# Layer 1 as seven products of quarters: W0 reloaded per batch, lora_a held still

## What is computed

```
Wc[b] = W0^T + I + coeff[b] * (2 * mask[b] - 1)         (1024 x 1024, per batch)
y[b]  = x[b] @ Wc[b] + b0                               (256 x 1024)
h[b]  = 2 * (y[b] @ lora_A[slot[b]])                    (256 x 16)
z[b]  = y[b] @ (W1^T + I) + b1 + h[b] @ lora_B[slot[b]] (256 x 1024)
```

## Time and profile before

| | |
|---|---|
| median of 3 runs | 392.09 us (392.07 to 392.19) |
| the profiled execution | 392.74 us |
| its span, first to last instruction | 390.9 us |
| instructions | 5982, of which 2334 matmuls |
| granted TensorE clock | 1.00 of full speed |
| moved by DMA | 61.76 MB, mean 158 GB/s |

### The profile page before, as it was taken

One profiled execution on the slowest core, in us unless ns is written; L12 is line 12 of the kernel. 1 busy time (PEld: TensorE's weight loads), 2 busy tenths in 40 slices (PEclk: granted clock), 3 DMA queues, 4 the chain that ended last, 5 costly groups with the idle time before them and its releaser, 6 DMA issues.

```text
span 390.9 us, 5982 instructions
## 1 busy us (share of the span) xinstructions
PE 382.0 (98%) x2334; PEld 359.1 (92%) x2334; DVE 245.9 (63%) x299; ACT 178.1 (46%) x313; POOL 49.7 (13%) x44
## 2 busy tenths in 40 slices
PE   8879999999999999999999999999999999999997
PEld 8879998998989999989999899899998999998996
DVE  3978989997177932788437981579617794281200
ACT  3546946656155622556235651464515563252221
POOL 2235910020003000030000300012000300002000
DMA  8999817873544633544526436164253562001011
GB/s 288 409 397 364 305 48 223 293 219 108 195 115 161 190 81 135 162 147 157 171 60 196 150 104 216 59 215 140 65 202 111 167 186 106 6 2 54 2 54 55
DMA packets 28078, 61.76 MB, mean 158 GB/s; under 512 B 2554, under 2 KB 3730, under 8 KB 28050
## 3 DMA queue, kind: packets, MB, share of 16 engines
q1 hardware_dynamic: 25232, 52.70, 41.6%
q10 hardware_dynamic: 2754, 8.66, 5.6%
q0 software_dynamic: 64, 0.01, 0.0%
HBM read 52.97 MB, written 8.39 MB: 157 GB/s over the span
## 4 chain that ended last, share of the span: by engine, by line
PE 83%; DVE 6%; DMA 4%; issue 3%; ACT 2%; SPq 1%; ACTq 0%; DVEq 0%
PE z_ps L385 43%; PE y_ps L347 23%; PE y_ps L353 12%; DMA ring<-in_mask 4%; DVE ring L680 3%; PE y_ps L385 2%; PE z_ps L429 2%; DVE wc_lo L688 2%; ACT wc_hi L499 1%; PE y_ps L317 1%; PE y_ps L327 1%; DVE y_two L727 0%; PE t_ps L420 0%; DVE y_raw L721 0%; ACT z_rows L552 0%
## 5 line engine op out<-in xcount | busy, mean ns | idle before, releaser
L385 PE MATMUL z_ps<-w_hi,y_two 128*128 128x344 f32 (+1 forms) x736 | 184.0, 323 | 1.3 <-DVE y_two L727 0.7
L385 PEld LDWEIGHTS z_ps<-w_hi,y_two 128*128 128x128 f32 x736 | 129.5, 188 | 3.0 <-DVE y_two L727 1.0
L347 PE MATMUL y_ps<-x_two,wc_hi 128*128 128x512 f32 x448 | 127.5, 395 | 0.0
L688 DVE SCALAR_TENSOR_TENSOR wc_lo<-ring,coeff_neg,wc_hi 128x1024 fp32r<-128x1024 f32 (+1 forms) x67 | 92.5, 1381 | 47.3 <-ACT wc_hi L499 46.5
L385 PE MATMUL z_ps<-w_lo,y_two 128*128 128x344 f32 (+1 forms) x368 | 118.3, 321 | 0.0
L499 ACT ACTIVATE wc_hi<-ring,coeff_neg 128x1024 fp32r<-128x1024 f32 (+1 forms) x67 | 74.6, 1115 | 71.5 <-PE y_ps L353 37.3
L680 DVE SCALAR_TENSOR_TENSOR ring<-ring,coeff_two,w_t 128x1024 f32<-128x1024 int32 (+1 forms) x67 | 86.6, 1301 | 8.2 <-DMA ring<-in_mask 7.3
L347 PEld LDWEIGHTS y_ps<-x_two,wc_hi 128*128 128x128 f32 x448 | 78.1, 189 | 10.9
L353 PEld LDWEIGHTS y_ps<-x_two,wc_lo 128*128 128x128 f32 x448 | 70.9, 189 | 8.4
L353 PE MATMUL y_ps<-x_two,wc_lo 128*128 128x256 f32 x448 | 78.2, 281 | 0.0
L385 PEld LDWEIGHTS z_ps<-w_lo,y_two 128*128 128x128 f32 x368 | 69.3, 188 | 0.0
(11 more groups left out here) (49 smaller groups left out, 182.3 us busy)
## 6 DMA issues: line engine op xcount, KB each, us to landing
ring<-in_mask SPq DMA_DIRECT2D x63, 512.0 KB, 4.4
x_raw<-in_x SPq DMA_DIRECT2D x31, 256.0 KB, 6.3
out<-z_rows ACTq DMA_DIRECT2D x15, 512.0 KB, 3.2
w_raw<-in_w SPq DMA_DIRECT2D x8, 512.0 KB, 10.3
w_t<-in_w SPq DMA_DIRECT2D x7, 512.0 KB, 9.3
b_raw<-in_lora_b SPq DMA_DIRECT2D x8, 256.0 KB, 3.6
w_t<-in_w SPq DMA_DIRECT2D x2, 256.0 KB, 3.7
ring<-in_mask SPq DMA_DIRECT2D x2, 256.0 KB, 4.8
```

The source lines that it names most:

```text
L347: pe.matmul(y_ps[o % HT][:, 0:2 * T], w, x_two[:, k, :, :], start=(k == 0), stop=False, skip_group_check=True)
L385: ins = pe.matmul(z_bank(b, s, g)[:, 0:EDGES[g + 1] - EDGES[g]], ys[:, k, s * P:(s + 1) * P], w[:, k, EDGES[g]:EDGES[g + 1]], start=(k == ...
L688: dve.scalar_tensor_tensor(out=wc_lo[:, k % RING, lo:hi], in0=sums[:, mask_entry(b, k) % RING, lo:hi], scalar=coeff_neg[:, b:b + 1], in1=w ...
```

## The change

- **Layer 1 from batch 2 on** (`winograd(b)`, FIRST = 2): y and W1 are cut in quarters of 128 or 512 by 512, and the four quarters of z are made of seven products instead of eight (Strassen's scheme in Winograd's form). Names: y quarters Y11, Y21, Y12, Y22, sums S1 = Y21 + Y22, S3 = Y11 - Y21, S2 = Y22 - S3, S4 = Y12 - S2; weight quarters W11 to W22 and T1 to T4, made once of quarters of W1 that are loaded again. V12 stands for the split Y12.
- **Batches 0 and 1** use plain products, but in halves of 512 columns (4 banks: 2 row halves x 2 column halves) instead of three groups.
- **h**: lora_a, high and low side by side, stands still (32 columns) and y moves, so h comes out turned (`low_rank`); `turn_h` and its copies are gone. In a seven-product batch h is made of Y11 with S1 times lora_a's upper half, Y12 times its lower half, and Y22 times their difference. lora_b is stacked seven times (112 rows) instead of four.
- **W0** isn't kept: each unit's piece of W0 is loaded with its mask into a ring of 6 slots, the sum is made in the mask's place, the high part in W0's place, the low part in the mask's. A slot is free when TensorE has used the unit; SP waits for that. Diagonals are raised for units 0, 1, 6 and 7 of every batch, two 128 x 128 blocks each.
- **PSUM**: two sets of four banks change places from half to half.
- **The lists** of all engines are written anew around this; `z_copy` of the seven-product batches becomes three `p_copy` on ScalarE, one `p_add` and four `z_add` on VectorE.

The diff, cut to its core (new functions as they are called):

```diff
-RING = 4
+RING = 6
@@ sync
-            def load_mask(b, k):
-                e = mask_entry(b, k)
+            def load_weights(b, k):
+
+                e = entry(b, k)
                 if e >= RING:
-
-                    sp.wait_ge(wc_lo_done, parts(0, e - RING))
+                    block_read(sp, b, k - RING)
...
+                    sp.dma_start(slot(w0_at, e), w0_u[:, ks, cols]).then_inc(w0_in[e % RING], 16)
+                    sp.dma_start(slot(mask_at, e), mask_u[b][:, ks, cols]).then_inc(ring_in[e % RING], 16)
...
             def load_x(b, g):
-                need(sp, x_lo_done, XG * (b - 1) + g + 1)
+                if b > 0:
+                    block_read(sp, b - 1, KT - 1)
...
+                need(sp, z_full, 4 * b)
+                sp.dma_start(b_raw[0:B_ALL, :], lora_b[bass.ds(slot, 1)].rearrange("a r o -> (a r) o")).then_inc(b_in, 16)
...
             for b in range(1, NB):
+                before = PAIR if b == 1 else HT
+                for u in range(before):
+                    load_weights(b, u)
                 for g in range(XG):
                     load_x(b, g)
...
+                for u in range(before, RING):
+                    load_weights(b, u)
+                if b == FIRST:
+
+                    sp.wait_ge(w12_read, 1)
+                    for c in range(2):
+                        load_t(T3, c, 1, W22, t_in[T3, c])
+                        load_t(T3, c, 0, W12, t_other_in[T3, c])
+                    load_lora(b)
+                if b == 1:
+
+                    for c in range(2):
+                        load_t(T1, c, 1, W12, t_in[T1, c])
+                        load_t(T1, c, 0, W11, t_other_in[T1, c])
+                        load_t(T2, c, 1, W22, t_in[T2, c])
+                        load_t(T4, c, 1, W21, t_in[T4, c])
+                    load_lora(b)
+                elif b > FIRST:
+                    load_lora(b)
+                for u in range(RING, KT):
+                    load_weights(b, u)
@@ gpsimd
+                w0_diagonal(b, KT - 2)
+                w0_diagonal(b, KT - 1)
+                if b + 1 < NB:
+                    w0_diagonal(b + 1, 0)
+                    w0_diagonal(b + 1, 1)
+                lora_a_diff(b)
                 lora_a_low(b)
-                lora_b_low(b)
+                lora_b_low(b, 0)
+                lora_b_low(b, 1)
@@ tensor
+            def product(bank, q, j, k, start):
+
+                for n, (yp, wp) in enumerate(((0, 0), (0, 1), (1, 0))):
+                    ins = pe.matmul(bank[:], y_two[:, q, k, yp, :], w1_two[wp][:, j, k, :],
+                                    start=(start and k == 0 and n == 0), stop=False, skip_group_check=True)
+                return ins
...
+            def low_rank(hs, q, a, k, start):
+                return pe.matmul(hs, a_parts[:, a, :, :], y_two[:, q, k, :, :], start=start, stop=False,
+                                 skip_group_check=True)
...
+                whole(X, Y11, W11, True).then_inc(p_full, 1)
+                pe.wait_ge(t_lo_done, t_count(T3, 1))
+                whole(V, S3, T3, True).then_inc(p_full, 1)
+                whole(W, V12, W21, True)
+
+                pe.wait_ge(p_copied, copied + 2)
+                whole(V, Y22, T4, False)
+                pe.wait_ge(y_lo_done, y_parts(b, S1))
+                pe.wait_ge(y_sum_done, KT * (b - 1) + HT + 1)
+                winograd_low_rank(b)
+
+                whole(Y, S1, T1, True).then_inc(p_full, 1)
+                pe.wait_ge(p_copied, copied + 1)
+                whole(X, S2, T2, False).then_inc(p_full, 1)
+                close(b, W)
+                close(b, V)
+
+                pe.wait_ge(y_lo_done, y_parts(b, S4))
+                pe.wait_ge(p_added, b - FIRST + 1)
+                for k in range(HT):
+                    product(layer1_bank(b, Y), S4, W22, k, False)
...
@@ scalar, batches from 2 on
+                    weights_high(b, KT - 2)
+                    store(b - 1, 0)
+                    store(b - 1, 1)
+                    for o in range(HT):
+                        y_copy(b, o)
+                    weights_high(b, KT - 1)
+                if winograd(b):
+                    y_high(b, Y11)
+                    y_high(b, S3)
...
                 lora_b_high(b)
+                lora_b_copy(b, 0)
                 if b + 1 < NB:
+                    weights_high(b + 1, 0)
+                    weights_high(b + 1, 1)
+                lora_a_high(b)
 
                 for o in range(HT, KT):
                     y_copy(b, o)
@@ vector, batches from 2 on
+                    weights_sum(b, KT - 2)
+                    weights_low(b, KT - 2)
+                    for o in range(HT):
+                        y_sum(b, o)
+                    weights_sum(b, KT - 1)
+                    y_add(b, S3)
+                    weights_low(b, KT - 1)
+                    y_low(b, Y11)
+                    y_low(b, S3)
                 if b + 1 < NB:
                     weights_sum(b + 1, 0)
+                    step(b + 1, 0)
+                    weights_low(b + 1, 1)
...
                 for o in range(HT, KT):
                     y_sum(b, o)
+                if winograd(b):
+                    y_add(b, S1)
+                    y_low(b, V12)
+                    y_add(b, S2)
+                    y_low(b, Y22)
+                    y_low(b, S1)
+                    y_add(b, S4)
+                    y_low(b, S2)
+                    y_low(b, S4)
+                    if b + 1 < NB:
+                        weights_sum(b + 1, PAIR)
+                        x_low(b + 1, 0)
+                        step(b + 1, PAIR)
+                        x_low(b + 1, 1)
+                        weights_low(b + 1, HT - 1)
+                    h_low(b)
+                    if b + 1 < NB:
+                        x_low(b + 1, 2)
+                        x_low(b + 1, 3)
+                    p_add(b)
+                    if b + 1 < NB:
+                        weights_sum(b + 1, HT)
+                        weights_sum(b + 1, HT + 1)
+                    z_add(b, W)
+                    if b + 1 < NB:
+                        weights_low(b + 1, HT)
+                    z_add(b, V)
+                    if b + 1 < NB:
+                        weights_low(b + 1, HT + 1)
+                    z_add(b, X)
+                    z_add(b, Y)
```

More of the change, by code:

```diff
@@ L34, in cond_residual_two_layers @@
     HALVED = 3
-    assert PAIR * T == BANK and PAIR == 2 and ST == 2 and XG == 4 and LR == 64 and KT == 2 * RING and NB > 2
+    FIRST = 2
+    B_HI, B_ALL = 6 * R, 7 * R
+    assert PAIR * T == BANK == HALF and PAIR == 2 and ST == 2 and XG == 4 and R == 16
+    assert HT < RING < KT and FIRST == 2 and NB > FIRST + 1
+    Y11, Y21, Y12, Y22 = range(4)
+    S1, S4, V12, S3, S2 = 1, 2, 4, 5, 6
+    Y_ORDER = (Y11, S3, V12, Y22, S1, S2, S4)
+    W11, W12, W21, W22, T1, T2, T4 = range(7)
+    T3 = W12
+    T_ORDER = ((T1, 0), (T2, 0), (T4, 0), (T1, 1), (T2, 1), (T4, 1), (T3, 0), (T3, 1))
     with ExitStack() as ctx:
@@ L73, in cond_residual_two_layers @@
[L73 to L78, removed]
+        a_raw = sb("a_raw", [P, KT + HT, R], F32)
+        a_parts = sb("a_parts", [P, KT + HT, 2, R], F32R)
+        h_stack = sb("h_stack", [P, T], F32R)
@@ L473, in layer1_last @@
-            def layer1_last(b):
-                layer1_group(b, 1, 2)
-                close_group(b, 1, 2)
+                for k in range(KT):
+                    if k == KT - 1:
+                        pe.wait_ge(y_lo_done, y_parts(0, k))
+                        plain_low_rank(0)
+                    pe.wait_ge(w1_lo_done, k + 1)
+                    pe.wait_ge(y_lo_done, y_parts(0, k))
+                    for i in range(4):
+                        plain(0, i, k)
+                for i in range(4):
+                    close(0, i)
@@ new lines, in z_copy, with store @@
+            def z_copy(b, i):
+                act.wait_ge(z_full, 4 * b + z_place(b, i))
+                s, _ = z_rows_of(b, i)
+                need(act, z_out[s], 16 * b)
+                act.activation(z_piece(b, i), layer1_bank(b, i)[:], ACT.Copy).then_inc(z_done, 1)
+            def store(b, s, lo=0, hi=D):
+                for i in range(4):
+                    rows, n = z_rows_of(b, i)
+                    if rows == s and lo <= n * HALF < hi:
+                        z_read(act, b, i)
@@ L653, in _ @@
-            store(NB - 1, 1, 0, 2)
-            z_copy(NB - 1, 1, 2)
-            store(NB - 1, 1, 2, 3)
+                    for t in (T1, T2, T4):
+                        t_high(t, 1)
+                    z_copy(b, 0)
+                    z_copy(b, 1)
+                    z_copy(b, 2)
+                    weights_high(b + 1, HT)
+                    z_copy(b, 3)
+                    t_high(T3, 0)
+                    t_high(T3, 1)
+                    weights_high(b + 1, HT + 1)
+            store(NB - 1, 0, 0, HALF)
```

815 lines of the change are left out of this document (495 added, 320 removed).

## The result

The median went from 392.08 us (391.87 to 392.19, 4 runs) to 397.96 (396.94 to 398.56, 4 runs): a ratio of 1.0148 with an interval of 1.0126 to 1.0170, so slower. I had forecast 387.8, range 383.8 to 396.5, with 0.67 on faster. The profiled execution took 398.56, its span 395.9. Lines (L556) are from here on those of the kernel after.

What follows compares the result with a forecast made beforehand. TensorE's matmul count times their pace was taken as the bound. From 392.74 us profiled, -8.6 + 2.5 + 1.3 + 0.5 = -4.3 gave 388.4, or 387.8 as median, range 383.8 to 396.5.

Steps and rivals of the forecast that it cites:

- TensorE's net, -8.6: Layer 1 on TensorE: -1.73 us in each of six seven-product batches, +1.0 in batch 1, +0.75 in batch 0.
- The wait at W: Layer 1, batches 2 to 6: TensorE wants V12 at 28.1, ready at 28.4; 0.5 us a batch, +2.5 in all.
- GpSimd's hold on VectorE: Ahead of V12 in a batch: four diagonal adds, lora_a and half of lora_b hold VectorE 2.7 us.
- Rival 2: VectorE's queue becomes the bound, from unit 6's low to V12's low; 2.5 us a batch, 397.8 us; chance 0.22.
- rival 1: No wait at W, y sums from PSUM perhaps not excluding GpSimd; 384 to 385 us; chance 0.22.
- Batch 1, +1.3: Batch 1's layer 0: late units 6 and 7 stall TensorE 2.3 us against 0.94; bounds -0.9 and +5.
- Batch 1's layer 0 starts at 61.7: End of batch 0: TensorE begins batch 1's layer 0 at 61.7 us.
- The landing: Batch 1's DMA queue: 14.2 MB by about 39 us, the other 15.2 MB at 386 GB/s, unit 7 landed at 78.5.
- rival 3: Batch 1 floods: T quarters queue ahead of units 6 and 7; up to 3.7 us more, 391.5 us; chance 0.12.
- The end, +0.5: From the last closing to the span's end: a 0.65 us sum and a 256 KB store instead of 172; +0.5 us.

Runs made afterwards that it cites:

- e10: e6 without GpSimd's identity adds for the weight units from batch 3, unit 6 on; 390.96 us, ratio 0.9956 to the kernel before.
- e1: The change as given, with batch 0's h brought forward on ScalarE and VectorE; 398.28 us, ratio 1.0161 to the kernel before.
- e4: e1 plus half of batch 1's T loads behind units 6 and 7, and three t_low behind batch 1's second y_low pairs; 394.96 us, ratio 1.0067.
- e11: e6 with batch 1's T loads, T passes and T diagonals moved behind what batch 1 itself needs; 388.68 us, ratio 0.9908 to the kernel before.
- e6: On e1 and e4's order, seven products from batch 3 on, T quarters spread over batches 1 and 2; 390.85 us, ratio 0.9968 to the kernel before.

## Why the prediction was wrong

**TensorE's net, -8.6: right.** The chain of waits of the kernel after shows a product's 24 matmuls and the 12 of h:

```profile
247.58 1.85 PE bank L567 x12
249.43 5.46 PE bank L556 x24
```

That is 227.5 ns a matmul and 19.1 us for 84, where I had 19.53 from the 232.5 of the earlier trace rows; h takes 1.85, not 1.88, so the 32-column stationary operand costs nothing that shows. A batch without a wait takes 44.54. The Trainium skill's rule ("TensorE: Matmul & The Clock Gate", Part 1, 215.7 ns at 512 columns) stays below this trace, by less than I had said.

**The wait at W: right in place and size, and lucky in what makes it up.** I had V12 done 28.4 us into the batch; in batch 4 W starts at 241.85 - 213.41 = 28.44, behind a wait of 0.36. The waits at W sum to 2.9 over four batches, against my 2.5 over five; batch 2 has 1.4 of it. But 2.7 of my 28.4 were GpSimd's hold on VectorE. VectorE's timeline of batch 4 has other things in their place:

```profile
222.36 1.28 DVE L919 SCALAR_TENSOR_TENSOR ring_raw<-ring_raw,coeff_two 128x1024 f32<-128x1024 int32 x1 [5.21 <-DMA ring_raw<-in_mask]
...
235.01 1.28 DVE L919 SCALAR_TENSOR_TENSOR ring_raw<-ring_raw,coeff_two 128x1024 f32<-128x1024 int32 x1 [1.44 <-DMA ring_raw<-in_mask]
```

Unit 6 is there 8.95 us into the batch, not 8.2, and ahead of the second half's y sums VectorE waits 1.44 for the mask of the next batch's second unit, a wait that my walk did not have (1.73, 1.44, 1.12 and 1.72 in batches 3 to 6). These two are 2.2 of the 2.7. In e10 VectorE waits for that mask as well (0.99, 1.86 and 1.61 in batches 4 to 6), which fits that the adds taken out gained nothing there. Rival 2 (VectorE the bound) did not happen: VectorE is busy 36.8 of 45.5 us, where I had 39.6; 1.6 or more of the difference are my 0.25 for each of 8 GpSimd adds, by e10 at most 0.05. Whether y sums and GpSimd exclude each other, rival 1's mechanism, these runs don't show.

**Batch 1, +1.3 with bounds -0.9 and +5: this is the step that failed**, together with the line that ends batch 0 ("Batch 1's layer 0 starts at 61.7", costed at no wait). Measured against the forecast they cost +5.2 and +5.0. By e1 they are one thing, since the first can be removed and the time stays. Three terms were mis-sized:
- *The landing.* I had unit 7 land at 78.5, so unit 6 at 75.8, one unit (1.05 MB) earlier. The chain shows

```profile
71.58 10.47 DMA ring_raw<-in_mask
```

 and VectorE's sum of unit 6 starts at 82.07, 6.3 us later. VectorE's timeline and two windows (columns as above) of the kernel after:

```profile
82.07 1.29 DVE L919 SCALAR_TENSOR_TENSOR ring_raw<-ring_raw,coeff_two 128x1024 f32<-128x1024 int32 x1 [6.35 <-DMA ring_raw<-in_mask]
...
0.00:39.00 39.00, 32.30 (x229) 31.02 (x230) 28.62 (x32) 19.10 (x26) 11.25 (x21) 0.96 0.97 343
39.00:82.05 43.05, 38.84 (x182) 31.73 (x181) 32.47 (x31) 21.04 (x30) 23.38 (x25) 0.96 1.05 377
```

 I had 28.3 MB moved by then, 14.2 of them by 39 (the kernel before has 365 GB/s there). 343 and 377 GB/s are 13.4 and 16.2, together 29.6 MB. The start was 0.8 MB behind (2.1 us at 377), 1.3 MB more passed than my list of transfers has (3.4 us), and 377 in place of 386 GB/s is 0.9 us; which transfers the 1.3 MB belong to the windows don't say. The queue's order I had right, and it was rival 3's; its 3.7 us were too little and its chance of 0.12 too small. A plain count: by the end of its layer 0 batch 1 must load W0 again, 4.2 MB that the kernel before did not, and 4.2 MB of T quarters (T3's 2.1 follow in batch 2).
- *The lists.* I walked batch 1 only to unit 7. The three t_low of 5 us stand ahead of the second half's y sums, and TensorE's h waits 2.36 for the y_low behind them (in e4, where they stand later, this wait is gone); in batch 0, h_high stands behind the high part of unit (1,2), whose sum is reached at 61.27. I had named rival 2 for such a run of VectorE, but looked for it only in steady state.
- *The clock.* After the wait of 4.21 the first 8 matmuls of layer 0 take 2.56 us and the next 8 take 1.74, where 1.40 is the pace; the granted clock reads 0.50 in the first stretch, the lower of its two levels, and 0.80 in the second. After the wait of 2.36, the 8 matmuls of h take 2.57 us, where 1.8 is the pace, and 24 more take 6.35, where 5.46 is, at 0.70 and 0.85. That is 1.5 and 1.6 us. After unit 7's wait the clock reads 1.00; 0.4 us more is lost there, since the low part of unit 7 is only done at 90.94. Of batch 1's 55.1 us, 47.3 is work (e11), 4.0 and 0.4 are waits, 3.1 or so the slower clock that follows them; 0.2 is left over. I had costed a wait at its own length.

**The end, +0.5: right.** From the last closing (392.33) to the span's end it takes 3.57 us, against 3.2 before, so +0.4.

So the parts that repeat, batches 2 to 6, were within 0.3 us in sum, and the one-time part, costed in a paragraph, decided the sign.

## What to carry to other kernels

A scheme that pays in steady state has an entry price; walk the first batches as closely as the repeating one, both the bytes ahead of each load in its queue and the list of each engine to its end. Where the memory is saturated, move one-time work not behind the next thing that waits but to where a whole batch of slack is, and start the new scheme a batch later if need be: here one plain batch more costs 1.6 us, and with it and the moves of e1 and e11 the version is 10 us faster than the change as given. A wait removed early shows nothing as long as a second one bounds the same stretch; test such waits in pairs.

## What was not expected of the hardware

- In these runs a wait of TensorE of 2.4 to 5.5 us is followed by matmuls at the lower clock: 8 matmuls in 2.56 us instead of 1.40 after 4.21, and a granted clock of 0.50 from 84 to 89 us after e1's 5.46, which costs 2.7 us more than the wait itself. After the wait of 1.67 the clock reads 1.00.
- GpSimd's 128-column adds cost VectorE at most 0.05 us each in steady state (e10), though in the start of the kernel before a pass beside one was 0.25 longer. y_low is longer all the same, 829 ns in the mean against 691 before, and in the stretch of e10's window it is 840 without the diagonal adds, where e11 has 840 and e6 859 with them. So it comes from something else that these runs don't show.
- With the queue saturated at 377 to 387 GB/s a mask lands as much as 10.5 us after issue, against 4.4 in the median before. In e11's batches 1 and 2 masks take 9.0 in the median, at 324 and 279 GB/s, and this cost TensorE nothing: lateness counted only for what was wanted soon.
